# Sums over a head's rows, taken for four recurrence steps at once in TensorE's four column groups

## The chip, the cores and the metric

The kernel runs on one core of a Trainium2 chip. The time is that of one execution on the device, in microseconds (us). Engines are named as the profile names them: PE (TensorE, matmuls) and PEld (its weight loads), DVE (VectorE), ACT (ScalarE), POOL (GpSimd), SP (the engine that issues most DMAs). They run beside each other, each through its own list of instructions in order, and wait for each other on semaphores.

## The reference, cut to what matters

Two layers; the change is in the attention part of the first, a recurrence over 1024 tokens of 4 sequences, with 256 channels in 16 heads of N = 16:

```
r, k, v = xr @ Wr, xk @ Wk, xv @ Wv;  g = silu(xg @ Wg)
decay = exp(-exp(tdecay + tanh(xw @ td_w1) @ td_w2))
def step(S, inp):                       # S: one N x N matrix (i, j) for each head
    r_t, k_t, v_t, d_t = inp
    kv = k_t[..., :, None] * v_t[..., None, :]
    y = einsum('bhi,bhij->bhj', r_t, S + u[None, :, :, None] * kv)
    return d_t[..., None] * S + kv, y
mu, var = yh.mean(-1), yh.var(-1)       # over the 16 channels j of a head
yn = (yh - mu) / sqrt(var + EPS) * ln_w + ln_b
out = (yn * g) @ Wo
```

The sum over i, for each head and each j, is what the change deals with, and the mean over j that follows it.

## The kernel before, in words

Data lie with channels on the 128 partitions (CC = 2 blocks of P = 128 channels, 8 heads each) and the T = 1024 tokens of one sequence along the free dimension. A matmul takes at most W = 512 tokens, so there are BPB = 2 halves. The B = 4 sequences are run one after the other. S is never kept as a matrix: for a fixed block c and a fixed j, row (head, i) of S over all tokens is a scan on the partition (head, i). So a sequence has NJ = 32 recurrence steps (2 blocks, 16 values of j), 128 in all, numbered s. A step is made of:

- PE, `spread(s)` (L1089): two f32r matmuls put v of channel (head, j) on the 16 partitions of its head, into PSUM banks 0 and 1 or 2 and 3. It waits until the scan of step s-2 is done.
- DVE: kv = k * that, in PSUM (L1445), then the scan over the tokens (L1449) into one of the buffers of `st` (`state`), a ring of RING = 3. With s >= 3 the scan waits for `y_mm`, the sum that freed its buffer.
- POOL: state times r, in place (L1350, `pr_done`).
- PE, `y_sum(s)` (L1101): two fp32 matmuls, one for each half, with weights `sum_j[:, j, :]` (128 x 128) that add the 16 rows of each head into that head's channel j of banks 4 and 5. They hold 1 - 1/N in that column and -1/N in the others of the head, so the 16 steps of a block leave y less its mean over the head. At j = 15 two matmuls with `centre` (L1107) add the bonus term u*r*k*v, centred too.

An fp32 matmul stands in the trace as two MATMUL records and two weight loads.

Around the steps stands the side work, through banks 6 and 7 in turn (`side`, in the order of `USES`; a use waits until the one two before it has been read): the layernorm and mixes of the next sequence (`mean`, `var`, `bcast`, `xx`, `t5`, `m`, `td1`, `p`, `td2`), and behind each block's sums its group norm: `y` (ACT copies banks 4 and 5 to `y_`, L1284, and their square to `gsq`, L1285), `gvar` (variance), `gb` (1/std spread to the channels), and `wo` (output projection). The list `A_STEPS` gives, by hand, what each engine does in step s after its own part; `beside(b, n)` says which side work stands at step n of a sequence. All engines follow the same list. In step s PE does `y_sum(s-2)`, then `spread(s+1)`, then the side work; DVE does kv(s), the scan(s), then the side work.

A channel block stands inside permuted: first by half of j, then by head, then by j in the half (`by_parts`).

Of the kernel before, what the change touches and what calls it, by code (L numbers as in the profile page):

```python
# [10 lines left out]
P = 128  # L11
CC = C // P
NT = B * T
W = 512
# [4 lines left out]

HEADS, N = 16, 16  # L20
TM, TD = 32, 64
GN_EPS = 1e-5 * 8 ** 2
# [62 lines left out]
def adaln_kernel(nc, a, out):  # L85
# [40 lines left out]
    with ctx:  # L126
# [40 lines left out]
        def phase(spec):  # L167
# [16 lines left out]
            ("v_", [P, CC, T], fp32), ("v_parts", [P, CC, 2, T], f32r), ("decay", [P, CC, T], fp32),  # L184
            ("g_", [P, 2, CC, T], fp32), ("y_", [P, CC, T], fp32), ("gsq", [P, T], fp32), ("state", [P, 3, T + 1], fp32),
# [4 lines left out]
            ("spread", [P, N // 2, P], f32r), ("sum_j", [P, N, P], fp32),  # L190
            ("head_parts", [P, P], fp32), ("ident_a", [P, P], fp32), ("mean_parts", [P, P], fp32), ("centre", [P, P], fp32),
# [757 lines left out]
        V_MAA_X, V_DECAY, V_U, V_LNW, V_LNB = 5, 6, 7, 8, 9  # L949
        MIXES, NJ, RING = 5, CC * N, 3  # L950
        HALF_N = N // 2
# [21 lines left out]
        def beside(b, n):  # L973


            todo = []
            if n == 0:
                todo += both("td2", b, 1)
            if n == 1:
                if b:  # L980
                    todo += [("y", b - 1, 1)]
                todo += [("split", b, 1)]
            if b:
                todo += {3: [("gvar", b - 1, 1)], 4: [("gb", b - 1, 1, 0)], 5: [("gb", b - 1, 1, 1)],
                         9: both("wo", b - 1, 0), 10: both("wo", b - 1, 1)}.get(n, [])
# [15 lines left out]
        A_STEPS += [(b * NJ + n, beside(b, n)) for b in range(B) for n in range(NJ)]  # L1001
        A_STEPS += [(B * NJ, []), (B * NJ + 1, [("y", B - 1, 1)]), (None, [("gvar", B - 1, 1)]),
                    (None, both("gb", B - 1, 1)), (None, both("wo", B - 1, 0) + both("wo", B - 1, 1))]


        def reader(what):

            if what[0] == "p":
                return "V" if MIX_ORDER[what[2]][what[3]] == MIX_G else "A"
            return {"mean": "V", "var": "A", "bcast": "V", "t5": "A", "m": "V", "td1": "A", "td2": "A", "gvar": "A",  # L1010
                    "gb": "V", "wo": "V", "bonus": "V"}.get(what[0])
# [24 lines left out]
        def by_parts(ap):  # L1036

            return ap.rearrange("p (h x j) -> p x h j", x=2, j=HALF_N)

# [24 lines left out]
        def pe_a(pe):  # L1064
# [16 lines left out]
            def spread(s):  # L1081
                b, n = divmod(s, NJ)
                c, j = divmod(n, N)
                if s >= 2:
                    pe.wait_ge(scan_done, s - 1)
                if j == 0:
                    pe.wait_ge(lo_done_a, (b * CC + c + 1) * 2)
# [5 lines left out]

            def y_sum(s):
                b, n = divmod(s, NJ)
                c, j = divmod(n, N)
# [7 lines left out]
                if j == N - 1:  # L1104
                    wait_read(pe, ("bonus", b, c, 1))
                    for half in range(BPB):
                        ins = nc.tensor.matmul(bank(4 + half), a_["centre"][:, :], y_[:, c, half * W:(half + 1) * W],  # L1107
                                               start=False, stop=True, skip_group_check=True)
                    ins.then_inc(y_full, 1)

            def use(what):
# [49 lines left out]
                elif kind == "bonus":  # L1161
                    _, _, c, h = what
                    pe.wait_ge(rk_done, b * CC + c + 1)
                    ins = nc.tensor.matmul(side(what), a_["head_u"][:, c, :], y_[:, c, h * W:(h + 1) * W], start=True, stop=True)
                elif kind == "gvar":
                    c = what[2]
                    pe.wait_ge(y_copied, b * CC + c + 1)
                    for t in range(BT):
                        ins = nc.tensor.matmul(side(what)[:, t * (P // N):(t + 1) * (P // N)], gsq[:, t * P:(t + 1) * P],
                                               a_["mean_parts"][:, 0:P // 2:HALF_N], start=True, stop=True, skip_group_check=True)  # L1170
                elif kind == "gb":
# [28 lines left out]
        def act_a(act, own):  # L1200
            act.wait_ge(a_loaded, 16 * N_A_LOADS)
            for n in ("wv", "wg"):
                for k in range(CC):
                    for c in range(CC):
                        ins = nc.scalar.activation(a_[n][:, k, c * P:(c + 1) * P].rearrange(
                            "p (x h j) -> p x h j", x=2, j=HALF_N), by_parts(a_[n + "_in"][:, k, c * P:(c + 1) * P]), ACT.Copy)
            ins.then_inc(perm_read, 1)
# [7 lines left out]
            def do(what):  # L1215
# [65 lines left out]
                elif kind == "y":  # L1281
                    c = what[2]
                    act.wait_ge(y_full, b * CC + c + 1)
                    nc.scalar.activation(y_[:, c, :], bank2(4), ACT.Copy)  # L1284
                    nc.scalar.activation(gsq[:, :], bank2(4), ACT.Square).then_inc(y_copied, 1)  # L1285
                elif kind == "gvar":
# [3 lines left out]
                elif kind == "gb" and what[3] == 0:  # L1290

                    c = what[2]
                    act.wait_ge(rstd_done, RSTD["gvar", b, c])
                    for x in range(2):
                        to = gsq[:, :].rearrange("p (t x h j) -> p t x h j", x=2, h=P // N, j=HALF_N)[:, :, x, :, :]
                        ins = nc.scalar.activation(to, a_["gn_rs"][:, :, :].unsqueeze(3).broadcast_to(
                            [P, BT, P // N, HALF_N]), ACT.Copy)
                    ins.then_inc(widened, 1)
                elif kind == "gb":
# [55 lines left out]
        def dve_a(dve, own):  # L1355
            dve.wait_ge(a_loaded, 16 * N_A_LOADS)
            dve.wait_ge(h_zero, 1)
            parts = dict(x=2, h=P // N, j=HALF_N)
            nc.vector.tensor_copy(a_["ident_parts"][:, :].rearrange("p (x h j) -> p x h j", **parts),
                                  by_parts(a_["ident_a"][:, :])).then_inc(maps_done, 1)  # L1360
            for x in range(2):
                nc.vector.tensor_copy(a_["ident_twice"][:, x * (P // 2):(x + 1) * (P // 2)].rearrange(
                    "p (h j) -> p h j", j=HALF_N), by_parts(a_["ident_a"][:, :])[:, 0, :, :]).then_inc(maps_done, 1)
            heads, in_parts = a_["head_ones"][:, 0:P:N], a_["head_parts"][:, :]
            own.link(nc.vector.tensor_copy(in_parts.rearrange("p (x h j) -> p x h j", **parts), by_parts(a_["head_ones"][:, :])))

            own.link(nc.vector.tensor_scalar(a_["sum_j"][:, :, :], in_parts.unsqueeze(1).broadcast_to([P, N, P]), -1.0 / N, None,
                                             ALU.mult))
            for j in range(N):
                first = j // HALF_N * (P // 2) + j % HALF_N  # L1370
                ins = nc.vector.tensor_scalar(a_["sum_j"][:, j, first:first + P // 2 - HALF_N + 1:HALF_N], heads, 1.0 - 1.0 / N, None, ALU.mult)
            ins.then_inc(fixed_done, 1)
# [62 lines left out]
            for s, todo in A_STEPS:  # L1435
                if s is not None and s < B * NJ:
# [1042 lines left out]
```

## Time and profile before

| | us |
|---|---|
| median of 3 runs | 5319.94 (5316.01 to 5320.66) |
| the profiled execution, its own time | 5312.82 |
| its span, first to last instruction | 5311.0 |
| granted clock of PE, mean | 0.953 |
| the 128 steps | from 178 to 853 |

The page of the profile gives busy time by engine and by slice of the span. The views by window, by group of instructions and in order of time give the stretch from 178 to 853 us, in which the recurrence stands. The rest of the span belongs to other parts of the two layers, which the change leaves as they are.

### The profile page before, as it was taken

What the parts mean: (1) busy time and instruction counts of PE and PEld (TensorE: products, weight loads), DVE (VectorE), ACT (ScalarE), POOL (GpSimd) and SP (SyncE); (2) the same over time, 40 slices, a digit from 0 to 9 for tenths busy, and PEclk for the clock granted to TensorE, in tenths of its full rate; (3) what the DMA queues carried; (4) which work ended last, traced back from release to release, by engine and by line L of the source; (5) the groups of instructions that cost most, each with busy time, mean ns of one, the idle gap of its engine ahead of it and who ended that gap; (6) DMA issues with size and microseconds to landing.
All of it is one profiled execution on the core that took longest, in us unless ns stands there. A gap on an engine that the chain in (4) does not pass through costs nothing. (4 is left out here: it accounts for less than half of the span.)

```text
span 5311.0 us, 84166 instructions
## 1 busy us (share of the span) xinstructions
PE 4578.8 (86%) x28586; PEld 2382.0 (45%) x28586; DVE 4038.4 (76%) x6600; ACT 3406.8 (64%) x2365; POOL 3149.1 (59%) x2722
## 2 busy tenths in 40 slices
PE   5999987786589988888898888898988888399999
PEld 3344443473234434344344343443443434277777
DVE  2688886524499999999999999999999998522221
ACT  1221211211599999999999999999999996334443
POOL 0566563420477777777777777777777774133333
PEclk8899998898799999999999999999999998699999
DMA  6000001351100000000000000000000000200000
GB/s 217 0 0 0 0 0 44 116 183 69 46 3 2 4 2 2 18 2 3 3 2 4 16 2 4 2 4 2 11 4 2 2 4 3 96 8 16 8 16 8
DMA packets 71211, 123.45 MB, mean 23 GB/s; under 512 B 8231, under 2 KB 46727, under 8 KB 68032
## 3 DMA queue, kind: packets, MB, share of 16 engines
q1 hardware_dynamic: 61888, 98.94, 5.6%
q0 software_dynamic: 9216, 23.17, 1.2%
q8 instruction: 57, 0.93, 0.1%
q14 instruction: 50, 0.41, 0.0%
HBM read 67.39 MB, written 61.03 MB: 24 GB/s over the span
## 5 line engine op out<-in xcount | busy, mean ns | idle before, releaser
L892 DVE CUSTOM_DVE_ANT_0 e_slots<-e_slots,banks 128x1024 f32<-128x1024 f32 x2048 | 2445.6, 1216 | 104.3 <-PE banks L577 99.9
L660 ACT ACTIVATE e_slots<-e_slots 128x4096 f32<-128x4096 f32 x512 | 1841.1, 3620 | 75.5 <-DVE e_slots L847 50.9
L577 PE MATMUL banks<-ex_parts,sel 128*128 128x512 f32 x4096 | 1520.4, 454 | 159.5 <-DVE ew L892 153.1
L536 PE MATMUL banks<-e_slots,w_score 128*32 128x256 f32 x16384 | 1256.2, 399 | 175.3 <-ACT e_slots L660 168.8
L744 POOL TENSOR_SCALAR e_slots<-k,qt 128x1024 f32<-128x1024 f32 x896 | 1002.9, 1121 | 672.4 <-DVE ew L892 631.2
L750 POOL TENSOR_SCALAR e_slots<-e_slots,qt 128x1024 f32<-128x1024 f32 x896 | 1000.3, 1124 | 64.5 <-POOL e_slots L744 25.7
L577 PEld LDWEIGHTS banks<-ex_parts,sel 128*128 128x128 f32 x4096 | 632.4, 190 | 904.3 <-DVE ew L892 733.2
L536 PEld LDWEIGHTS banks<-e_slots,w_score 128*32 128x32 f32 x16384 | 375.9, 110 | 873.0 <-issue 567.6
L651 ACT ACTIVATE e_slots<-k,qt 128x1024 f32<-128x1024 f32 x512 | 570.6, 1139 | 4.6 <-DVE ew L892 4.4
L2190 POOL TENSOR_TENSOR g_l<-tmp,g_h 128x512 fp32r<-128x512 f32 x192 | 248.8, 1296 | 437.4 <-ACT g_h L2157 307.0
L847 DVE TENSOR_SCALAR e_slots<-k,qt 128x1024 f32<-128x1024 f32 x640 | 466.3, 792 | 0.5 <-POOL qt L754 0.5
L1350 POOL TENSOR_TENSOR state<-state,r_ 128x1024 f32<-128x1024 f32 x128 | 290.0, 2267 | 223.6 <-DVE state L1449 223.2
L2070 PE MATMUL banks<-g_h,r_h 128*128 128x512 f32 x1024 | 410.3, 401 | 0.9 <-POOL g_l L2190 0.9
L2070 PE MATMUL banks<-g_l,r_h 128*128 128x512 f32 x1024 | 404.4, 395 | 0.0
L1449 DVE TENSOR_TENSOR_SCAN state<-decay,banks 128x1024 f32<-128x1024 f32 x128 | 292.7, 2287 | 4.4
L1101 PE MATMUL banks<-state,sum_j 128*128 128x512 f32 x512 | 255.2, 621 | 37.3 <-POOL state L1350 31.4
L2156 ACT ACTIVATE tmp<-banks,r_sh 128x512 f32<-128x512 f32 x128 | 88.2, 689 | 267.8 <-PE banks L2070 267.7
L2237 DVE SCALAR_TENSOR_TENSOR xr<-banks,r_s3g,xr 128x512 f32<-128x512 f32 x16 | 11.3, 747 | 269.1 <-PE banks L2070 269.1
L2070 PEld LDWEIGHTS banks<-g_h,r_h 128*128 128x128 f32 x1024 | 192.2, 188 | 51.0 <-issue 3.3
L2070 PEld LDWEIGHTS banks<-g_l,r_h 128*128 128x128 f32 x1024 | 192.2, 188 | 49.3 <-issue 3.3
L667 ACT ACTIVATE ex<-banks,negmax 128x512 f32<-128x512 f32 x128 | 88.2, 689 | 185.6 <-DVE negmax L864 185.6
L2216 DVE RECIPROCAL r_std<-r_std 128x512 f32<-128x512 f32 x8 | 26.8, 3353 | 224.9 <-ACT r_std L2126 224.9
(313 smaller groups left out, 5234.3 us busy)
## 6 DMA issues: line engine op xcount, KB each, us to landing
moe_slots<-empty_slot SPq DMA_DIRECT2D x1, 10320.0 KB, 47.3
slots<-moe_slots SPq DMA_DIRECT2D x8, 1290.0 KB, 6.3
moe_out<-empty_slot SPq DMA_DIRECT2D x1, 8192.0 KB, 67.9
two_rows<-moe_out SPq DMA_DIRECT2D x16, 512.0 KB, 6.5
stage<-in_h SPq DMA_DIRECT2D x8, 1024.0 KB, 4.8
x_tokens<-in_x SPq DMA_DIRECT2D x1, 4096.0 KB, 13.9
w_down<-in_w_down SPq DMA_DIRECT2D x1, 4096.0 KB, 12.3
x_between<-x_tokens SPq DMA_DIRECT2D x8, 512.0 KB, 4.8
```

Of the source, the lines that this page charges most:

```text
L536: ins = nc.tensor.matmul(banks[TI * g:TI * (g + 1), par, side * QW:(side + 1) * QW], c_["w_score"][:, s, half, :], e_slots[:, par, COLG * ...
L577: ins = nc.tensor.matmul(spread[n % 2][:, half * W:(half + 1) * W], c_["sel"][:, half, n, :], ex_parts[:, par, :], start=True, stop=True)
L651: nc.scalar.activation(e_slots[:, par, n, :], k2[:, :], ACT.Relu, bias=qt[:, par, 0, place(n):place(n) + 1]).then_inc(z_a, 1)
L660: nc.scalar.activation(e_slots[:, par, four, :], e_slots[:, par, four, :], ACT.Sqrt, bias=EPS_RHO).then_inc(sqrt_done, 1)
L744: nc.gpsimd.tensor_scalar(e_slots[:, par, n, :], k2[:, :], FLT_MAX, qt[:, par, 1, place(n):place(n) + 1], ALU.min, ALU.max).then_inc(z_cla ...
L750: nc.gpsimd.tensor_scalar(e, e, qt[:, par, 0, place(n):place(n) + 1], 1.0, ALU.add, ALU.mult).then_inc(z_p, 1)
L847: nc.vector.tensor_scalar(e_slots[:, par, n, :], k2[:, :], qt[:, par, 0, place(n):place(n) + 1], 0.0, ALU.add, ALU.max).then_inc(z_v, 1)
L892: nc.vector.tensor_tensor_reduce(out=e, in0=e, in1=spread[n % 2], scale=1.0, scalar=0.0, op0=ALU.mult, op1=ALU.add, accum_out=ew[:, q, pla ...
L1101: ins = nc.tensor.matmul(bank(4 + half), a_["sum_j"][:, j, :], st[:, s % RING, half * W:(half + 1) * W], start=j == 0, stop=False, skip_gr ...
L1350: nc.gpsimd.tensor_tensor(state, state, r_[:, b % 2, n // N, :], ALU.mult).then_inc(pr_done, 1)
L1449: nc.vector.tensor_tensor_scan(st[:, s % RING, 1:T + 1], dk[:, c, :], kv, 0.0, ALU.mult, ALU.add).then_inc(scan_done, 1)
L2070: ins = nc.tensor.matmul(dst, w_[w][:, k, o * P:(o + 1) * P], x[:, k, :], start=k == 0 and part_ == 0, stop=k == n_k - 1 and part_ == 1)
```

## The change

- `RING` goes from 3 to 6. `sum_j` (128 x 16 x 128) is replaced by `sum_4` (128 x 4 x 4 x 8): weights of 32 columns, ones in the 8 columns of slot i, for i from 0 to 3.
- The 16 values of j are taken in the order 0, 4, 8, 12, 1, 5, 9, 13, ... (`J_ORDER`), so that four steps in a row belong to the four quarters of the j.
- `y_sum` is replaced by `y_sums`, which runs after every fourth step. For each half it issues four fp32 matmuls, one for each of the four steps' states, of 32 output columns each, into partitions 0-31, 32-63, 64-95 and 96-127 of bank 4 or 5. The scan waits for the sum of its ring's group of four.
- The permuted order of channels becomes j first, then head. The set-up copies, `ident_parts`, `mean_parts`, and the widening of `gn_rs` (one ACTIVATE of 1024 instead of two of 512) follow it.
- The sums no longer take away the mean. The bonus term is added with `ident_a` instead of `centre`, and a new side use `cen` (two for each block) multiplies the copied y with `centre`; ACT takes the square of the result into `gsq` and copies it back to `y_`. `y` is now one ACTIVATE. `cen` stands at steps 2 and 18; `gvar` moves from 3 and 19 to 4 and 20, `gb` from 4, 5, 20, 21 to 5, 6, 21, 22.

```diff
+RING = 6
-"state", [P, 3, T + 1]            -"sum_j", [P, N, P]
+"state", [P, RING, T + 1]         +"sum_4", [P, 4, 4, P // N]
...
+        GROUP = 4
+        J_ORDER = [N // GROUP * g + i for i in range(N // GROUP) for g in range(GROUP)]
...
-                todo += {3: [("gvar", b - 1, 1)], 4: [("gb", b - 1, 1, 0)], 5: [("gb", b - 1, 1, 1)],
+                todo += {2: both("cen", b - 1, 1), 4: [("gvar", b - 1, 1)], 5: [("gb", b - 1, 1, 0)], 6: [("gb", b - 1, 1, 1)],
...
-                     17: [("y", b, 0)], 19: [("gvar", b, 0)], 20: [("gb", b, 0, 0)], 21: [("gb", b, 0, 1)]}.get(n, [])
+                     17: [("y", b, 0)], 18: both("cen", b, 0), 20: [("gvar", b, 0)], 21: [("gb", b, 0, 0)], 22: [("gb", b, 0, 1)]}.get(n, [])
...
-            return ap.rearrange("p (h x j) -> p x h j", x=2, j=HALF_N)
+            return ap.rearrange("p (h j) -> p j h", j=N)
...
-            def y_sum(s):
+            def y_sums(s):
...
                 pe.wait_ge(pr_done, s + 1)
-                if j == 0 and s:
+                if i == GROUP - 1 and s >= N:
                     pe.wait_ge(y_copied, s // N)
+                onto = a_["sum_4"][:, i // GROUP, :, :].rearrange("p i h -> p (i h)")
                 for half in range(BPB):
-                    ins = nc.tensor.matmul(bank(4 + half), a_["sum_j"][:, j, :], st[:, s % RING, half * W:(half + 1) * W],
-                                           start=j == 0, stop=False, skip_group_check=True)
+                    for g in range(GROUP):
+                        ins = nc.tensor.matmul(banks[g * 32:(g + 1) * 32, 4 + half, :], onto,
+                                               st[:, (s - GROUP + 1 + g) % RING, half * W:(half + 1) * W],
+                                               start=i == GROUP - 1, stop=False, skip_group_check=True)
                 ins.then_inc(y_mm, 1)
...
-                        ins = nc.tensor.matmul(bank(4 + half), a_["centre"][:, :], y_[:, c, half * W:(half + 1) * W],
+                        ins = nc.tensor.matmul(bank(4 + half), a_["ident_a"][:, :], y_[:, c, half * W:(half + 1) * W],
...
+                elif kind == "cen":
+                    _, _, c, h = what
+                    pe.wait_ge(y_copied, b * CC + c + 1)
+                    ins = nc.tensor.matmul(side(what), a_["centre"][:, :], y_[:, c, h * W:(h + 1) * W], start=True, stop=True)
                 elif kind == "gvar":
-                    pe.wait_ge(y_copied, b * CC + c + 1)
+                    wait_read(pe, ("cen", b, c, 1))
...
-                if s is not None and s >= 2:
-                    y_sum(s - 2)
+                if s is not None and s >= 2 and (s - 2) % GROUP == GROUP - 1:
+                    y_sums(s - 2)
...
-                    nc.scalar.activation(y_[:, c, :], bank2(4), ACT.Copy)
-                    nc.scalar.activation(gsq[:, :], bank2(4), ACT.Square).then_inc(y_copied, 1)
+                    nc.scalar.activation(y_[:, c, :], bank2(4), ACT.Copy).then_inc(y_copied, 1)
+                elif kind == "cen":
+                    _, _, c, h = what
+                    cols = slice(h * W, (h + 1) * W)
+                    wait_mm(act, what)
+                    nc.scalar.activation(gsq[:, cols], side(what), ACT.Square)
+                    nc.scalar.activation(y_[:, c, cols], side(what), ACT.Copy).then_inc(side_a, 1)
...
+            own.link(nc.vector.memset(a_["sum_4"][:, :, :, :], 0.0))
+            for i in range(4):
+                ins = nc.vector.tensor_copy(a_["sum_4"][:, i, i, :], heads)
...
                     if s >= RING:
-                        dve.wait_ge(y_mm, s - RING + 1)
+                        dve.wait_ge(y_mm, (s - RING) // GROUP + 1)
```

## Rows read from the trace of the kernel before

**Rows 1.** The page: busy time by engine over the whole span.
```profile
PE 4578.8 (86%) x28586; PEld 2382.0 (45%) x28586; DVE 4038.4 (76%) x6600; ACT 3406.8 (64%) x2365; POOL 3149.1 (59%) x2722
```

**Rows 2.** By window: length, busy by engine (instructions), clock, DMA share, GB/s.
```profile
178.00:853.00 675.00, 611.26 (x1675) 283.10 (x1675) 561.08 (x413) 138.38 (x193) 421.72 (x187) 0.96 0.00 0
...
820.00:840.00 20.00, 14.25 (x35) 6.31 (x36) 19.83 (x12) 0.00 (x0) 13.34 (x7) 1.00 0.00 0
```

**Rows 3.** DVE's groups, 178 to 853: busy, mean ns, idle before, releaser.
```profile
L1449 DVE TENSOR_TENSOR_SCAN state<-decay,banks 128x1024 f32<-128x1024 f32 x128 | 292.7, 2287 | 4.4
L1445 DVE TENSOR_TENSOR banks<-k_,banks 128x1024 f32<-128x1024 f32 x128 | 155.5, 1215 | 9.2 <-PE banks L1089 9.2
L1406 DVE SCALAR_TENSOR_TENSOR xmix<-banks,vecs,xx 128x512 f32<-128x512 f32 x60 | 44.6, 748 | 30.2 <-PE banks L1140 21.3 <-PE banks L1142 6.5
...
L1427 DVE TENSOR_TENSOR y_<-y_,banks 128x512 f32<-128x512 f32 x14 | 9.4, 672 | 16.6 <-PE banks L1176 16.6
L1432 DVE SCALAR_TENSOR_TENSOR x_tokens<-banks,mod,x_tokens 128x512 f32<-128x512 f32 x12 | 8.9, 742 | 9.6 <-PE banks L1182 9.6
L1413 DVE SCALAR_TENSOR_TENSOR g_<-th_g,banks 128x512 f32<-128x512 f32 x12 | 8.2, 687 | 18.0 <-ACT th_g L1248 18.0
L1386 DVE TENSOR_TENSOR xmix<-x_tokens,banks 128x1024 f32<-128x1024 f32 x6 | 7.3, 1221 | 12.4 <-PE banks L1116 12.4
L1393 DVE TENSOR_TENSOR xmix<-xmix,banks 128x1024 f32<-128x1024 f32 x6 | 7.3, 1212 | 6.0 <-PE banks L1126 6.0
...
L1390 DVE RECIPROCAL ln_rs<-ln_sd 128x4 f32<-128x4 f32 x6 | 1.1, 178 | 9.9 <-ACT ln_sd L1222 9.9
```

**Rows 4.** In order of time: a step with `p`, then one with `m`.
```profile
310.39 1.03 PE L1089 MATMUL banks<-v_parts,spread 128*128 128x512 f32 x2
...
311.26 3.60 PE L1155 MATMUL banks<-xmix,wv 128*128 128x512 f32 x8
...
314.70 1.88 PE L1101 MATMUL banks<-state,sum_j 128*128 128x512 f32 x4
...
316.97 1.98 PE L1140 MATMUL banks<-t5a,w2r 32*128 32x512 f32 x4
...
318.13 1.61 DVE L1406 SCALAR_TENSOR_TENSOR xmix<-banks,vecs,xx 128x512 f32<-128x512 f32 x2 [1.39 <-PE banks L1140]
...
324.60 1.88 PE L1101 MATMUL banks<-state,sum_j 128*128 128x512 f32 x4
```

**Rows 5.** In order of time: a step with no side work.
```profile
825.27 2.37 POOL L1350 TENSOR_TENSOR state<-state,r_ 128x1024 f32<-128x1024 f32 x1 [1.45 <-DVE state L1449]
...
826.34 2.29 DVE L1449 TENSOR_TENSOR_SCAN state<-decay,banks 128x1024 f32<-128x1024 f32 x1
...
827.68 1.98 PE L1101 MATMUL banks<-state,sum_j 128*128 128x512 f32 x4 [1.36 <-POOL state L1350]
...
829.79 2.29 DVE L1449 TENSOR_TENSOR_SCAN state<-decay,banks 128x1024 f32<-128x1024 f32 x1
```

**Rows 6.** PE's groups by line, whole run: the sums.
```profile
L1101 PE MATMUL banks<-state,sum_j 128*128 128x512 f32 x512 | 255.2, 621 | 37.3 <-POOL state L1350 31.4 <-ACT gsq L1285 5.6
```

**Rows 7.** In order of time, second layer: matmuls of 32 columns in four column groups.
```profile
2500.46 0.64 PE L536 MATMUL banks<-e_slots,w_score 128*32 128x256 f32 x8
2501.03 0.74 PE L577 MATMUL banks<-ex_parts,sel 128*128 128x512 f32 x2
```

**Rows 8.** In order of time: PE waits for POOL, then its clock is down.
```profile
739.26 3.78 PE L1101 MATMUL banks<-state,sum_j 128*128 128x512 f32 x4 [2.68 <-POOL state L1350]
742.05 1.84 PE L1089 MATMUL banks<-v_parts,spread 128*128 128x512 f32 x2
...
745.23 0.69 DVE L1427 TENSOR_TENSOR y_<-y_,banks 128x512 f32<-128x512 f32 x1 [4.26 <-PE banks L1176]
```

**Rows 9.** In order of time: one `g_` pair, waits of DVE.
```profile
341.81 0.69 DVE L1413 SCALAR_TENSOR_TENSOR g_<-th_g,banks 128x512 f32<-128x512 f32 x1 [1.03 <-ACT th_g L1248]
```

**Rows 10.** In order of time: the square behind the last step.
```profile
856.44 1.02 ACT L1285 ACTIVATE gsq<-banks 128x1024 f32<-128x1024 f32 x1
```

More of the change, by code:

```diff
@@ L184, in adaln_kernel @@
             ("v_", [P, CC, T], fp32), ("v_parts", [P, CC, 2, T], f32r), ("decay", [P, CC, T], fp32),
-            ("g_", [P, 2, CC, T], fp32), ("y_", [P, CC, T], fp32), ("gsq", [P, T], fp32), ("state", [P, 3, T + 1], fp32),
+            ("g_", [P, 2, CC, T], fp32), ("y_", [P, CC, T], fp32), ("gsq", [P, T], fp32), ("state", [P, RING, T + 1], fp32),
             ("t5a", [P, W], fp32), ("t5b", [TM, W], fp32), ("tw", [TD, BPB, W], fp32), ("th_g", [P, CC, W], fp32),
@@ L189, in adaln_kernel @@
             ("wg", [P, CC, C], fp32), ("wo", [P, CC, C], fp32), ("vecs", [P, 10, CC], fp32),
-            ("spread", [P, N // 2, P], f32r), ("sum_j", [P, N, P], fp32),
+            ("spread", [P, N // 2, P], f32r), ("sum_4", [P, 4, 4, P // N], fp32),
             ("head_parts", [P, P], fp32), ("ident_a", [P, P], fp32), ("mean_parts", [P, P], fp32), ("centre", [P, P], fp32),
@@ L949, in adaln_kernel @@
         V_MAA_X, V_DECAY, V_U, V_LNW, V_LNB = 5, 6, 7, 8, 9
-        MIXES, NJ, RING = 5, CC * N, 3
+        MIXES, NJ = 5, CC * N
+        GROUP = 4
+        J_ORDER = [N // GROUP * g + i for i in range(N // GROUP) for g in range(GROUP)]
         HALF_N = N // 2
@@ L1001, in adaln_kernel @@
         A_STEPS += [(b * NJ + n, beside(b, n)) for b in range(B) for n in range(NJ)]
-        A_STEPS += [(B * NJ, []), (B * NJ + 1, [("y", B - 1, 1)]), (None, [("gvar", B - 1, 1)]),
+        A_STEPS += [(B * NJ, []), (B * NJ + 1, [("y", B - 1, 1)]), (None, both("cen", B - 1, 1) + [("gvar", B - 1, 1)]),
                     (None, both("gb", B - 1, 1)), (None, both("wo", B - 1, 0) + both("wo", B - 1, 1))]
@@ L1009, in reader @@
                 return "V" if MIX_ORDER[what[2]][what[3]] == MIX_G else "A"
-            return {"mean": "V", "var": "A", "bcast": "V", "t5": "A", "m": "V", "td1": "A", "td2": "A", "gvar": "A",
+            return {"mean": "V", "var": "A", "bcast": "V", "t5": "A", "m": "V", "td1": "A", "td2": "A", "cen": "A", "gvar": "A",
                     "gb": "V", "wo": "V", "bonus": "V"}.get(what[0])
@@ L1082, in spread @@
                 b, n = divmod(s, NJ)
-                c, j = divmod(n, N)
+                c, i = divmod(n, N)
+                j = J_ORDER[i]
                 if s >= 2:
                     pe.wait_ge(scan_done, s - 1)
-                if j == 0:
+                if i == 0:
                     pe.wait_ge(lo_done_a, (b * CC + c + 1) * 2)
@@ L1164, in use @@
                     ins = nc.tensor.matmul(side(what), a_["head_u"][:, c, :], y_[:, c, h * W:(h + 1) * W], start=True, stop=True)
+                elif kind == "cen":
+                    _, _, c, h = what
+                    pe.wait_ge(y_copied, b * CC + c + 1)
+                    ins = nc.tensor.matmul(side(what), a_["centre"][:, :], y_[:, c, h * W:(h + 1) * W], start=True, stop=True)
                 elif kind == "gvar":
                     c = what[2]
-                    pe.wait_ge(y_copied, b * CC + c + 1)
+                    wait_read(pe, ("cen", b, c, 1))
                     for t in range(BT):
                         ins = nc.tensor.matmul(side(what)[:, t * (P // N):(t + 1) * (P // N)], gsq[:, t * P:(t + 1) * P],
-                                               a_["mean_parts"][:, 0:P // 2:HALF_N], start=True, stop=True, skip_group_check=True)
+                                               a_["mean_parts"][:, 0:P // N], start=True, stop=True, skip_group_check=True)
                 elif kind == "gb":
@@ L1205, in act_a @@
                         ins = nc.scalar.activation(a_[n][:, k, c * P:(c + 1) * P].rearrange(
-                            "p (x h j) -> p x h j", x=2, j=HALF_N), by_parts(a_[n + "_in"][:, k, c * P:(c + 1) * P]), ACT.Copy)
+                            "p (j h) -> p j h", j=N), by_parts(a_[n + "_in"][:, k, c * P:(c + 1) * P]), ACT.Copy)
             ins.then_inc(perm_read, 1)
@@ L1293, in do @@
                     act.wait_ge(rstd_done, RSTD["gvar", b, c])
[L1294 to L1298, printed above, removed]
+                    nc.scalar.activation(gsq[:, :].rearrange("p (t j h) -> p t j h", t=BT, j=N), a_["gn_rs"][:, :, :].unsqueeze(2)
+                                         .broadcast_to([P, BT, N, P // N]), ACT.Copy).then_inc(widened, 1)
                 elif kind == "gb":
@@ L1357, in dve_a @@
             dve.wait_ge(h_zero, 1)
-            parts = dict(x=2, h=P // N, j=HALF_N)
-            nc.vector.tensor_copy(a_["ident_parts"][:, :].rearrange("p (x h j) -> p x h j", **parts),
+            nc.vector.tensor_copy(a_["ident_parts"][:, :].rearrange("p (j h) -> p j h", j=N),
                                   by_parts(a_["ident_a"][:, :])).then_inc(maps_done, 1)
@@ L1362, in dve_a @@
                 nc.vector.tensor_copy(a_["ident_twice"][:, x * (P // 2):(x + 1) * (P // 2)].rearrange(
-                    "p (h j) -> p h j", j=HALF_N), by_parts(a_["ident_a"][:, :])[:, 0, :, :]).then_inc(maps_done, 1)
+                    "p (j h) -> p j h", j=HALF_N), by_parts(a_["ident_a"][:, :])[:, 0:HALF_N, :]).then_inc(maps_done, 1)
             heads, in_parts = a_["head_ones"][:, 0:P:N], a_["head_parts"][:, :]
[L1365 to L1371, printed above, removed]
+            own.link(nc.vector.tensor_copy(in_parts.rearrange("p (j h) -> p j h", j=N), by_parts(a_["head_ones"][:, :])))
+            own.link(nc.vector.memset(a_["sum_4"][:, :, :, :], 0.0))
+            for i in range(4):
+                ins = nc.vector.tensor_copy(a_["sum_4"][:, i, i, :], heads)
             ins.then_inc(fixed_done, 1)
```

4 lines of the change are left out of this document (2 added, 2 removed).

## The prediction

> **What bounds the kernel now.** I began with the page [rows 1]: PE is the busiest engine over the whole span. That says little here, because the change touches one stage only. The view by window gives that stage, the 128 steps, as 675 us [rows 2]: PE is busy for 611.3 us of them (91%), DVE for 561.1 (83%), POOL for 421.7 (62%), ACT for 138.4 (21%). The clock is at 0.96 and no DMA runs. So two engines are close to the bound, and the question is which of them ends the steps.
>
> The view in order of time answers it twice. With no side work, one scan starts 3.45 us after the other (826.34 to 829.79), which is the scan's 2.29 and the product's 1.22 and nothing between them [rows 3, 5]: DVE is the bound, and the sums (1.98 us) lie beside it. With side work it is the other way round. The sum of one step starts at 314.70 and the same one of the next pair at 324.60, so a pair of steps with a `p` and an `m` takes 9.9 us, and in it DVE waits 1.39 us for the matmuls of `m` [rows 4]. PE has no gap in that pair. I work its time out from starts: the `p` matmuls run from 311.26 to 314.70, so eight records take 3.44 us, 0.43 each. Four records (a sum, an `m`) then take 1.72, two (a spread) 0.86. The pair is 2 x 1.72 (sums) + 2 x 0.86 (spreads) + 1.72 (`m`) + 3.44 (`p`) = 10.3 us, near those 9.9. DVE's work for the pair is 2 x 3.50 + 2 x 0.75 = 8.5 us.
>
> So the end of the stage is DVE's: its 561.1 us of work plus 113.9 us of idle time. The groups by line say what it waited for [rows 3]: `m` 30.2, `g` 18.0, `gb` 16.6, `mean` 12.4, `ln_rs` 9.9, `wo` 9.6, the products 9.2, `bcast` 6.0 and 2 for the rest. Most of them are matmuls of the side work that stand in PE's list behind a `y_sum`. The change can give back no more than this idle time, since it takes no work from DVE inside the steps.
>
> **The change, part by part.**
>
> *The sums.* Before, 128 steps x 4 records x 0.43 = 220 us of PE. After, 32 calls of `y_sums`, each with 16 records of 128x512 on 32 columns. The nearest row is a matmul of the second layer with the same 32 columns, fp32 too, four column groups in a row: eight records of 256 elements start at 2500.46, and the next matmul starts at 2501.03, 0.57 us on [rows 7]. One after the other they would have taken 8 x 0.215 = 1.7 (half of the 0.43 of 512 elements each). So the groups do run together. At 512 elements I add two passes of 0.215 for the longer rows (1.0 us a half) or double the whole (1.14). A call is thus 2.0 to 2.3 us, and I take 2.3; the bound on the other side is 16 x 0.43 = 6.9 us, if nothing overlaps. 32 x 2.3 = 74 us, so 146 us leave PE.
>
> The Trainium skill, "TensorEngine Tiling (Array Packing)", Performance Considerations, promises up to four times for output columns of 32 or fewer, and its Key Properties say that a change of tiling mode drains the engine. Without any such drain a call would be 1.72 us and with it about what I take; the trace's 0.57 in place of 0.43 for the eight records agrees with a cost of this kind.
>
> *Waits of the sums.* Each `y_sum` waits for POOL's product, and `spread` and the side work are queued behind it on PE. PE lost 31.4 us that way and 5.6 us to the copy of the banks [rows 6]; once, POOL was late behind its `split`, PE stood 2.68 us, and DVE then 4.26 us at `gb` [rows 8]. Afterwards three steps in four have no such wait. In the fourth the order is the same as before. In a step without side work, POOL's product is ready about 2.5 us after its scan (827.68 less the scan's end at 825.2) [rows 5]; with 2.3 for the call and 0.86 for the spread that makes 5.7 us, and the product that needs the spread is due after 6.9. So the burst fits, with 1.2 us to spare. The ring of six adds no wait of its own: scan 4k+6 waits for the call that PE issues ahead of the very spread that its product needs.
>
> *`cen`.* Eight blocks x 4 records x 0.43 = 14 us more on PE, and for ACT four ACTIVATEs of 512 elements in place of one of 1024, at 21% busy. The bonus matmul keeps its size and only gets other weights. In the steps PE's sum is 611 - 146 + 14 = 479 us. On the chain, `cen` stands between `y` and `gvar`, which is moved one step later, where it meets `t5`; `gb` follows in steps that have `m` work. I put 0 to 2 us on each of the 8 blocks and take 2.5 in all. No DMA and no other queue is moved past.
>
> *Behind the last step* nothing covers `cen`. It adds 0.86 and some 0.3 of latency, and two times two ACTIVATEs of about 0.6 (half of 1.02, with its fixed part), and takes away the square of 1024 elements, 1.02 [rows 10]: 1 to 4 us, I take 3.
>
> *Set-up.* The fill of `sum_j` on DVE goes. It lay beside PE's permutations and the load of x, which end later, so it is worth nothing, with 0 to 1 us lost if the new strided copies on ACT are slower.
>
> *What DVE still waits for.* In the `p` and `m` pair PE now has 10.3 - 3.44 + half of 2.3 = 8.0 us against DVE's 8.5, so DVE bounds it. `m` keeps 8 of 30 (behind `t5`, and beside `wo`). `g`: the second of each pair waits for two matmuls and the tanh whatever PE did before, 1.03 in the row [rows 9], six pairs; with something for the first, 7.5 of 18 stay. `gb` 6 of 16.6. `mean` 3 of 12.4. `ln_rs` 5 of 9.9, as a chain of square, `var` and a table load is longer than one step. `wo` 6 of 9.6: around it four steps hold 22.6 us of PE against 20.2 of DVE. The products 8 of 9.2, since 7.7 of it is the very first start. `bcast` 2 of 6.0, the rest its 2, and 2.5 come new with `cen`. These are judged, not measured; together 50 stay and 64 go.
>
> *The clock.* Now PE is busy 14.25 of 20 us even where there is no side work, and the clock is 1.00 [rows 2]. After the change only a spread (0.86) stands in three of four such steps of 3.45 us. Where PE had stood for 2.68 us behind small matmuls the four records took 3.78 instead of 1.98 us and the spread 1.84 instead of 1.03 [rows 8]: the lower level, 1.2 GHz. I expect that in the stretches without side work. At 1.2 GHz a call takes 4.6 at most and a spread 1.72, so 2.5 + 4.6 + 1.7 = 8.8 against 6.9: a stall of 1 to 2 us in each group of four. About five groups of the last sequence and one in each of the others stand so: 8 x 1.5 = 12 us, or none if the clock holds. I take 10.
>
> "TensorE: Matmul & The Clock Gate", HAM oscillation, in the Trainium skill speaks against the change in the same way: gaps in PE's work send it to half rate. By it the stretches named would all be slow and the sum as I have it; without it, 10 us better.
>
> **Sum:** -64 + 10 + 3 = -51 us. Against the profiled execution's own 5312.8 us that is 5261.8. The median of the runs is 7.1 us above that execution, so the forecast is 5269 us for the median.
>
> **Rivals.**
> - *All waits go.* DVE runs without idle time but for the first start and the tail: 114 - 8 - 9 (its other fixed chains, `g` above all) = 97 less 3, so about 5226. For: in the last plain steps it does just that. Against: the chains over ACT. A gain between this and mine, 5226 to 5250, has a good chance.
> - *The waits are the chains' own.* If the side work of each step is late from its own round trip over ACT and POOL and not from the sum ahead of it, only the 37 us of PE's waits [rows 6] come through, in part: some 20 to 25 us, 5297. Against: PE has no gap in the pair of rows 4.
> - *The four column groups don't run together.* With 512 elements in two banks, or because the two records of an fp32 matmul follow each other in the same group, a call takes up to 6.9 us. From 3.5 us (6.9 - 2.5 - 0.86) it decides against DVE's pace in plain steps; at 6.9 each call holds DVE for 3.3 us there, about 10 groups, 33 us; PE's sum rises by 14 for `cen`, which it passes on where it is the bound; with 3 for the tail, about +45: 5365. This is the slower case. Against it stands the 0.57 of [rows 7]; 6%. At half overlap, 3.5 to 4.5 us, nothing changes in sign.
> - *A clock that stays down* also where there is side work would put 16 us of PE against 8.5 in a pair. The records of such a pair run at 0.43 each, the upper level, where PE is busy without a gap [rows 4], and in the pair it stays 94% busy; so at most in parts, a gain of 10 us or none: 5310.
>
> **How the numbers follow.** My forecast with its neighbourhood (5250 to 5288): 0.48. A larger gain (5220 to 5250): 0.22. Chains' own waits (5288 to 5309): 0.16. Clock down or small gain (5309 to 5331): 0.07. Slower (above 5331): 0.07. 0.2% is 10.6 us, about what a measurement of this kernel can tell from no change: faster below 5309.3, 0.86; the same 0.07; slower 0.07. The range takes 5222 to 5305, which leaves out 0.02 below and some 0.17 above.
>
> **What would show it.** The 128 steps take about 615 us (603 to 640 by the range). DVE's busy time in them stays near 561 and its idle time falls to about 55. A call of `y_sums` has 16 records in 2.0 to 2.3 us at full clock. `m` waits nearly vanish, and the second wait of each `g_` pair stays at 1.0. PE's clock falls below 0.9 in the last sequence. Wrong would be: a call above 3.5 us, DVE's product waiting for its spread behind a call in most groups, scans waiting for `y_mm`, or new waits at `gb` above 2 us a block.

## The result, and the profile after

The changed kernel takes 5339.36 us in the median of 7 runs (5331.51 to 5348.01), the kernel before 5320.66 (5310.2 to 5323.65) on the same chip: a ratio of 1.0037, with a 95% interval of 1.0026 to 1.0049. It is slower by 0.4%, where 1% faster was forecast. On another chip it was 1.0029 (1.0017 to 1.0040). The profiled execution, the slowest of the seven, has a span of 5346.3 us against 5311.0. 10.9 of those 35.3 us lie behind phase B's first matmul, in the part that the change leaves alone; no run says why.

First the stage by window, as in [rows 2]; the stretches go from the first scan's start to the last one's end, for the whole stage and for the last sequence alone. The kernel after:

```profile
184.70:868.90 684.20, 534.60 (x1688) 228.60 (x1686) 560.12 (x413) 153.86 (x213) 421.24 (x186) 0.82 0.00 0
...
732.20:868.90 136.70, 87.51 (x297) 38.07 (x296) 117.50 (x77) 17.32 (x23) 84.43 (x38) 0.71 0.00 0
```

The kernel before, the same two stretches:

```profile
178.20:849.30 671.10, 608.81 (x1670) 282.16 (x1669) 560.91 (x412) 138.38 (x193) 419.38 (x186) 0.96 0.00 0
...
722.30:849.30 127.00, 101.00 (x288) 48.53 (x287) 117.11 (x77) 15.08 (x19) 84.07 (x38) 0.97 0.00 0
```

DVE's work is the same (560.9 and 560.1 us) and the stage is 13.1 us longer, so all of the loss there is idle time of DVE. PE lost 74 us of busy time, not the 132 forecast. The clock column says why: 0.96 became 0.82, and in the last sequence 0.97 became 0.71. The last sequence, which has little side work, is 9.7 us longer although PE has less to do in it.

From here on I measure a version, in one profiled execution, by the distance between the starts of its first and its last scan: 668.8 us before (sequences 175.8, 184.0, 184.3 and 124.7), 681.9 after (176.3, 184.3, 186.8 and 134.5). A second profile of the changed kernel gave 680.5 us, with sequences up to 2.6 us apart, so a difference of that size between two versions says nothing. Two more pieces stand around the steps: the first scan starts at 184.7 instead of 178.2, and from the last scan's start to phase B's first matmul it is 38.0 instead of 33.2 us.

The call of `y_sums` is near what was forecast (2.0 to 2.3 us). In order of time, one at full clock and one in the last sequence:

```profile
304.42 1.93 PE L1108 MATMUL banks<-state,sum 128*32 128x512 f32 x16
...
843.14 3.64 PE L1108 MATMUL banks<-state,sum 128*32 128x512 f32 x16 [1.79 <-POOL state L1364]
...
846.71 1.82 PE L1094 MATMUL banks<-v_parts,spread 128*128 128x512 f32 x4
...
847.97 1.23 DVE L1456 TENSOR_TENSOR banks<-k_,banks 128x1024 f32<-128x1024 f32 x1 [1.01 <-PE banks L1094]
```

Sixteen records of 32 columns take 1.93 us, so the four groups do run together: apart they would take 6.9. At the lower level they take 3.64, and then the spread behind them is late and DVE waits 1.01 us for it.

DVE's idle time by group, to be laid beside [rows 3]:

```profile
L1456 DVE TENSOR_TENSOR banks<-k_,banks 128x1024 f32<-128x1024 f32 x128 | 155.5, 1215 | 14.4 <-PE banks L1094 14.4
L1417 DVE SCALAR_TENSOR_TENSOR xmix<-banks,vecs,xx 128x512 f32<-128x512 f32 x60 | 44.5, 747 | 32.3 <-PE banks L1148 27.6 <-PE banks L1150 3.2
...
L1438 DVE TENSOR_TENSOR y_<-y_,banks 128x512 f32<-128x512 f32 x14 | 9.4, 669 | 7.0 <-PE banks L1188 7.0
...
L1424 DVE SCALAR_TENSOR_TENSOR g_<-th_g,banks 128x512 f32<-128x512 f32 x12 | 8.1, 682 | 13.4 <-ACT th_g L1260 13.4
L1397 DVE TENSOR_TENSOR xmix<-x_tokens,banks 128x1024 f32<-128x1024 f32 x6 | 7.3, 1221 | 21.2 <-PE banks L1124 21.2
```

`gb` gave back 9.6 us, as meant, and `g` 4.6 of the 10.5 meant. But `mean` went from 12.4 to 21.2, the products from 9.2 to 14.4, `bcast` from 6.0 to 9.0, and `m`, which should have given back 22, stands at 32.3 where it had 30.2. `gn_rs`, the reciprocal behind `gvar`, went from 1.3 to 7.3 and `ln_rs` from 9.9 to 13.1. The scan itself waits 4.4 us in all before and after, so the ring of six and its waits for `y_mm` cost nothing.

### The profile page after: what moved, and what is told of

Read it like the earlier page. It is cut to its first block and busy times, and to the rows that moved or that the text cites. A ratio compares the mean times of both kernels' runs of the same rounds, so it can differ in the third digit from the quotient of the medians.

```text
span 5346.3 us, 84253 instructions
## 1 busy us (share of the span) xinstructions
PE 4522.7 (85%) x28618; PEld 2334.6 (44%) x28618; DVE 4036.7 (76%) x6588; ACT 3425.0 (64%) x2387; POOL 3151.5 (59%) x2722
## 5 line engine op out<-in xcount | busy, mean ns | idle before, releaser
L1094 PE MATMUL banks<-v_parts,spread 128*128 128x512 f32 x256 | 114.6, 536 | 91.3 <-DVE state L1460 86.1
## 6 DMA issues: line engine op xcount, KB each, us to landing
x_tokens<-in_x SPq DMA_DIRECT2D x1, 4096.0 KB, 14.1
```

## What the two traces suggest

**The clock (theory C).** `mean` stands at the head of a sequence, behind three steps with hardly any work for PE. In order of time, the kernel after:

```profile
356.52 1.21 PE L1094 MATMUL banks<-v_parts,spread 128*128 128x512 f32 x2 [2.71 <-DVE state L1460]
...
359.96 1.22 PE L1094 MATMUL banks<-v_parts,spread 128*128 128x512 f32 x2 [2.24 <-DVE state L1460]
...
361.11 3.78 PE L1168 MATMUL banks<-tw,td 64*128 64x512 f32 x4
...
364.82 3.78 PE L1124 MATMUL banks<-x_tokens,ones_mean 128*128 128x512 f32 x4
...
368.64 1.22 DVE L1397 TENSOR_TENSOR xmix<-x_tokens,banks 128x1024 f32<-128x1024 f32 x1 [5.29 <-PE banks L1124]
```

PE issued two records and then stood for 2.2 to 2.7 us, in each of these steps, and four records of `td2` and of `mean` now take 3.78 us each, against 1.98 before the change. DVE waits 5.29 us for the second. Before the change the sums filled those gaps. Theory C says that the freed PE pays for itself with a low clock, and more work on PE would be faster.

**The order (theory Q).** `cen` and the moved `gvar` and `gb` put new round trips on the chains. Step 23 takes 9.4 to 10.1 us from scan to scan, against 6.15 before:

```profile
315.35 1.24 ACT L1316 ACTIVATE y_<-y_,ln_half 128x1024 f32<-128x1024 f32 x1 [10.74 <-DVE y_ L1438]
...
316.53 0.75 DVE L1417 SCALAR_TENSOR_TENSOR xmix<-banks,vecs,xx 128x512 f32<-128x512 f32 x1 [1.21 <-PE banks L1148]
316.61 1.28 ACT L1251 ACT_TABLE_LOAD   x1
...
317.90 0.59 ACT L1251 ACTIVATE tw<-banks 64x512 f32<-64x512 f32 x1
318.55 1.64 PE L1148 MATMUL banks<-t5a,w2r 32*128 32x512 f32 x2 [2.06 <-ACT tw L1251]
...
320.22 0.75 DVE L1417 SCALAR_TENSOR_TENSOR xmix<-banks,vecs,xx 128x512 f32<-128x512 f32 x1 [2.94 <-PE banks L1148]
```

The second `gb` now shares step 22 with `td1`. ACT can take `td1`'s result only after its affine step, which waits for DVE's `gb`, and after a table load of 1.28 us; the bank that it holds is the one that the second `m` matmul needs. So DVE waits for PE, PE for ACT, and ACT for DVE, 4.2 us of DVE in all. Theory Q says that this order is the loss, and that a freed PE is worth what was forecast.

## The experiments

Where an experiment adds work, it is this: fp32 matmuls of 128x512 with zero weights, added into banks 4 and 5, so that the sums stay as they are.

**The part alone: three of four sums left out of the kernel before.** No `cen`, the old order; the output lacks those terms.

```diff
             def y_sum(s):
...
+                if j % 4 != 3:
+                    return
                 pe.wait_ge(pr_done, s + 1)
...
-                        dve.wait_ge(y_mm, s - RING + 1)
+                        dve.wait_ge(pr_done, s - RING + 1)
+                        if s - RING + 1 >= 4:
+                            dve.wait_ge(y_mm, (s - RING + 1) // 4)
```

> The kernel before the change with the sums of three of four steps left out (j = 3, 7, 11, 15 remain, two matmuls of 128x512 each, as before), so y lacks three quarters of its terms; no cen, the old order, a ring of three. It shows what freeing PE of the sums does alone. C: the clock of the steps falls to 0.80 to 0.87 and first to last scan only from 669 to 645 to 665 us, time 5295 to 5315. Q: DVE's waits behind the sums go, scans over 605 to 625 us, time 5255 to 5275, as forecast for the whole change.

Measured: 5313.2 us, 1.0004 (0.9994 to 1.0013) of the kernel before. The view by window, whole stage and last sequence:

```profile
176.90:842.10 665.20, 526.51 (x1288) 249.88 (x1286) 558.02 (x412) 138.94 (x193) 418.43 (x186) 0.79 0.00 0
709.00:842.10 133.10, 83.78 (x193) 43.27 (x192) 117.62 (x77) 15.19 (x19) 84.01 (x38) 0.69 0.00 0
```

PE is rid of 192 matmuls, and nothing comes of it: 662.9 us from first to last scan, 5.9 less than before, and the last sequence takes 130.8 instead of 124.7. Q's forecast of 5255 to 5275 is out; C's scans and time came true, with a clock of 0.79 just under its 0.80 to 0.87. This is the plainest answer to where the gain went, since the rest of the change is not in this kernel.

**The changed kernel with its sums apart.** Each step's sum in its own step, in one column group.

```diff
-                if s is not None and s >= 2 and (s - 2) % GROUP == GROUP - 1:
+                if s is not None and s >= 2:
...
+                g = i % GROUP
                 for half in range(BPB):
-                    for g in range(GROUP):
+                    ins = nc.tensor.matmul(banks[g * 32:(g + 1) * 32, 4 + half, :], onto,
+                                           st[:, s % RING, half * W:(half + 1) * W],
+                                           start=i < GROUP, stop=False, skip_group_check=True)
```

> The changed kernel, but each step's sum is issued in its own step as before the change, as two fp32 matmuls of 32 columns in one column group, so no four run together; cen, the order and the ring of six stay. C: PE is as busy as before the change, the clock is above 0.93, and the time is that of before plus 14 us of PE for cen and 3 for the tail, 5325 to 5335, with scans over 670 to 680. Q: the order costs as it does in the changed kernel and PE's sums come on top, 5350 or more, scans over 695 or more.

Measured: 5340.64 us, 1.0055 (1.0038 to 1.0072), clock 0.95 in the stage, 687.2 us from first to last scan. It lies between the two forecasts: the time is above C's and the scans below Q's 695. Against the kernel before, this version has as many records for the sums (of 32 columns now), the new set-up and order of j, the ring, `cen` and its order, at nearly the same clock (0.95 and 0.96), and its scans need 18.4 us more. 9.1 us of that are step 23 of the first three sequences, and 5.2 the last sequence. So both theories hold a part. Taking the sums together then saves 5.3 us (687.2 to 681.9), about the 5.9 of the part alone.

**The old order.** `gvar` and `gb` back at their steps, `cen` where it is.

```diff
-                todo += {2: both("cen", b - 1, 1), 4: [("gvar", b - 1, 1)], 5: [("gb", b - 1, 1, 0)], 6: [("gb", b - 1, 1, 1)],
+                todo += {2: both("cen", b - 1, 1), 3: [("gvar", b - 1, 1)], 4: [("gb", b - 1, 1, 0)], 5: [("gb", b - 1, 1, 1)],
...
-                     17: [("y", b, 0)], 18: both("cen", b, 0), 20: [("gvar", b, 0)], 21: [("gb", b, 0, 0)], 22: [("gb", b, 0, 1)]}.get(n, [])
+                     17: [("y", b, 0)], 18: both("cen", b, 0), 19: [("gvar", b, 0)], 20: [("gb", b, 0, 0)], 21: [("gb", b, 0, 1)]}.get(n, [])
```

> The changed kernel with gvar and gb put back to the steps at which they stood before the change (gvar 3 and 19, gb 4, 5, 20, 21; cen stays at 2 and 18). C: no change that matters, 5335 to 5345, clock 0.82. Q: the waits at step 23 (9.4 to 10.1 us from scan to scan, 6.15 before the change) go back to about 6, 3.5 us in each of three sequences, and the time falls by 10 to 15 us to about 5326.

Measured: 5315.49 us, 1.0006 (0.9996 to 1.0015), the same as the kernel before; 665.3 us from first to last scan, 16.6 less than the changed kernel, at the same clock of 0.82. Step 23 takes 4.76 us in each of the three sequences, 15.0 us less in all. The other steps of those three are 2.5 us longer together, and the last sequence, which has no `td1`, is 4.2 us shorter. So the collision is most of what the order costs, and not all. DVE's wait for `m` falls from 32.3 to 19.5 us and the one at `gn_rs` goes; the one at `gb` rises from 7.0 to 10.8. Q is right on the order, by more than it said.

**PE filled in every step.** Two zero-weight matmuls at the end of PE's step, in the three of four steps without a call.

```diff
+            def fill(s, halves):
+                start = (s - 2) % N < GROUP - 1
+                for half in range(halves):
+                    nc.tensor.matmul(bank(4 + half), a_["zero_w"][:, :], a_["wo"][:, :, :].rearrange("p k c -> p (k c)"),
+                                     start=start, stop=False, skip_group_check=True)
...
                         use(what)
+                if s is not None and 2 <= s < B * NJ and (s - 2) % GROUP != GROUP - 1:
+                    fill(s, 2)
```

> The changed kernel, with two fp32 matmuls of 128x512 with zero weights into banks 4 and 5 at the end of PE's step in each step that has no call of y_sums (nothing is left out; zeros are added). It gives PE back about the busy time that the change took from it, but behind the side work instead of ahead of it. Theory C (the clock: PE, freed, falls to 1.2 GHz and its matmuls on DVE's chains take twice as long): the granted clock of the 128 steps rises from 0.82 to above 0.93, first to last scan falls from 682 to 640 to 655 us, and the time is 5290 to 5315. Theory Q (the order of the side work: cen, and gvar and gb moved onto steps with t5 and td1): the clock rises too, but the scans stay at 680 or more and the time at 5335 to 5350.

Measured: 5378.5 us, 1.0126 (1.0109 to 1.0143), and 719.7 us from first to last scan. C's 5290 to 5315 is out, and the time is above Q's 5350 too, but the sequences differ. The first three take 597.7 us instead of 547.4: DVE's wait for `m` rises from 32.3 to 58.9 us and that for `gb` from 7.0 to 19.0, while the products wait less (11.0 for 14.4). The added matmuls stand in PE's list ahead of the next step's side work. The last one takes 122.0 us instead of 134.5:

```profile
774.60:898.90 124.30, 105.49 (x392) 46.94 (x390) 116.78 (x77) 17.21 (x23) 84.52 (x38) 0.97 0.00 1
```

PE has 18 us more to do in it than in the changed kernel, the clock is 0.97 instead of 0.71, and it is 12.4 us shorter. That suggests that the fill has to stand in the gaps only, which the next version tries.

**PE filled in light steps only.** The same call under one more condition: the side work of the step has less than 1 us for PE (steps 3, 30 and 31 of a sequence, and most of the last). `PE_US` is a table of the side work's PE time: `p`, `wo`, `t5`, `mean`, `td1` 1.7 us, `var`, `gvar` 1.8, `bcast`, `gb` 1.1, `m`, `cen`, `bonus`, `td2` 0.86.

```diff
-                if s is not None and 2 <= s < B * NJ and (s - 2) % GROUP != GROUP - 1:
+                if (s is not None and 2 <= s < B * NJ and (s - 2) % GROUP != GROUP - 1
+                        and sum(PE_US.get(w[0], 0) for w in todo) < 1.0):
```

> The changed kernel with the two zero-weight fp32 matmuls of 128x512 at the end of PE's step only where PE has next to no side work (steps 3, 30 and 31 of a sequence and most of the last sequence), nothing left out. In the run with them in all steps the last sequence took 122.0 us between scans against 134.5 in the changed kernel, and the first three 597.7 against 547.4. C (the low clock costs time by itself): the last sequence takes 120 to 126 us, the first three fall to 535 to 545 because mean and the first uses of a sequence meet a warm PE, and the time is 5315 to 5328. Q (only the order costs; more PE work can only delay): the last sequence stays above 130, time 5335 or more.

Measured: 5311.29 us, 1.0000 (0.9991 to 1.0010); 659.0 us from first to last scan, sequences 173.7, 182.1, 183.5 and 119.7. That is 22.9 us less than the changed kernel, by added work alone. The clock of the last sequence is 0.94, and the idle time ahead of `mean` fell from 21.2 to 11.8 us. C holds, with a time 4 us better than its range.

**Light steps filled, and the old order**, the last edit and that of the old order together.

> The same zero-weight matmuls in light steps, with gvar and gb at their old steps (5315.5 without the matmuls). C: the two gains add, last sequence 118 to 124, time 5292 to 5305, faster than the kernel before the change. Q: 5312 to 5320, as without them.

Measured: 5297.68 us, 0.9981 (0.9971 to 0.9991); 649.1 us from first to last scan. The time is in C's range. Of the two gains, 16.6 and 22.9 us, 32.8 are there together: they add in the main, and not wholly.

**The steps with `m`, `cen` or `bonus` alone filled too** (the bound 1.0 becomes 1.8).

> As the one before, with zero-weight matmuls also in the steps whose only side work on PE is the two matmuls of m, cen or bonus (1.7 us). C, if the low clock also holds the m and p steps: 5285 to 5300, below the light version. If PE's own order is tight there, as in the run with them in all steps: 5305 to 5325, above it. Q: above 5315.

Measured: 5286.76 us, 0.9955 (0.9938 to 0.9971): 0.45% faster than the kernel before, within C's range. First to last scan 640.5 us, clock 0.92:

```profile
177.10:819.90 642.80, 565.28 (x1876) 243.26 (x1874) 558.89 (x412) 145.50 (x207) 418.94 (x186) 0.92 0.00 1
```

**The part alone, with light steps filled.** The kernel before with three of four sums left out (as above, so its output lacks them) and the matmuls of zero weight.

> The kernel before the change with three of four sums left out (y lacks those terms; 5313.2) and the zero-weight matmuls in light steps. It asks what the freed PE is worth when the clock is held in the light steps. C: last sequence from 130.8 back to 118 to 124, the first three from 532 to 515 to 525, time 5285 to 5300. Q, or chains over ACT and POOL as the limit: 5308 to 5318.

Measured: 5287.42 us, 0.9955 (0.9941 to 0.9969), against 1.0004 without the fill. First to last scan 643.4 instead of 662.9; the last sequence 122.4 instead of 130.8. What frees PE is worth 5.9 us on this stage when the clock is left to itself and 25.4 us when it is held up in the light steps. The kernel before as it is, with the same fill, was not run; its clock in the stage is 0.96 already, but what the fill would give there is open.

**The changed kernel again, and a fill ahead of the first scan.** The first scan's start had fallen on two values: 175.5 to 178.2 in the kernel before and five versions, 184.0 to 185.3 in the changed kernel and three versions. (The expectation below miscounts them.)

> The changed kernel once more, on the chip that also runs the next one. Before its first scan it issues the same matmuls in the same order as the kernel before the change; the first scan stood at 178.2 us there, at 184.7 in it, and in seven variants at 175.5 to 178.0 four times... and at 184.0 to 185.3 three times, in both families. If that is the chance of where the clock rises, this run may show either value and no other; if it belongs to the change's set-up, it is 184 to 185 again. Time 5325 to 5345 by both theories.

Measured: 5334.66 us; first scan at 175.0, first to last scan 680.5. So the first scan's 6.5 us are no part of the change, and its loss in the stage repeats, 11.7 us after 13.1.

```diff
+                if s is None and todo[0][0] in ('mean', 'xx') and todo[0][1] == 0:
+                    for k in range(1 if todo[0][0] == 'mean' else 3):
+                        fill(2, 1)
```

> The best version so far (gvar and gb at their old steps, zero-weight matmuls in light and middling steps, 5286.8) with the same kind of matmul also ahead of the first scan: one behind each of the first two mean and three behind each of the first two xx, where PE waits 2 to 6 us and the clock is 0.77. C: the low clock costs time there too; first scan at 168 to 174 us instead of 175 to 185, time 5275 to 5283. If those matmuls only get in the way: first scan at 180 or later, 5288 or more.

Measured: 5293.06 us, 0.9948 (0.9930 to 0.9965), with the chip's kernel before at 5319. The first scan starts at 171.1, and the clock from 60 us to there is 0.88 instead of 0.72 to 0.78. The first scan's start is what C said. The time is not: 5293 misses the expected 5275 to 5283 by 10 us, where the kernel before is slower by 6 on this chip. In the profile the scans take the 640.5 us of the version without this fill, and the part behind phase B's first matmul, with no fill in it, is 13.7 us longer; that is left open. In ratio it is the fastest version, but its interval overlaps that of the other.

## Why the prediction was wrong

**What bounds the stage**: right. DVE's 561 us of work stayed (560.1), and time was won and lost in its idle time alone.

**The sums**: right. A call takes 1.93 us, under the 2.0 to 2.3 of the forecast.

Three terms of the sum failed. For the stage it had -64 for the waits and +10 for the clock, -54 us, and the profile showed +13.1. Of the 67.1 us between them, 14.8 are the clock's (24.8 that the fill gives back, less the 10), 16.6 the order's, and 35.7 are left for the waits, with `cen` and the rest of the low clock in them.

**The clock, sized too small.** Its direction and its mechanism were right, its size and its reach wrong. I priced it at 10 us, in stretches without side work, by calls that delay their spread. The last sequence alone is 9.8 us longer, but 5.2 of that stand in the version with the sums apart too, at a clock of 0.95. What I left out is that the same low clock is carried into the work behind a light stretch: DVE's wait at `mean`, at the head of each sequence, rose from 12.4 to 21.2 us, and light steps filled bring it back to 11.8. Those records take twice as long (3.78 us for 1.98), and DVE waits for them. With the light and middling steps filled the stage falls by 24.8 us (665.3 to 640.5), and with the light ones alone by 22.9, 16.2 and 19.5 us in three kernels. So the term was 16 to 25 us, where I had 10. It is probably more, since the clock was still 0.92 and the fill takes PE's time; no run held the clock at 0.96 with the sums together. From the Trainium skill, "TensorE: Matmul & The Clock Gate", HAM oscillation, I had weighed against the change that gaps in PE's work bring it to half rate. The trace agrees, with 3.64 us for a call in the last sequence, though the page tells of longer waits, for DMA, and here gaps of 2.2 to 2.7 us went with the lower level.

**`cen` and the order, sized too small.** "0 to 2 us on each of the 8 blocks and take 2.5 in all" was 18.4 us at nearly equal clock (the version with the sums apart), of which the order is 16.6 (the old order). Most of it is one collision, three times, `gb` and `td1` in step 22. I had looked at `gvar` beside `t5` and had not followed who holds the two side banks: I counted PE's time for each step, and the loss is a chain through three engines, one after the other; ACT's three instructions alone are 3.1 us of it. Behind the last step the piece is 4.8 us longer, where I took 3. Both the clock and `cen` have a part in it. Without `cen` it takes 33.2 us in the kernel before and 32.9 in the filled version, with the clock in it at 0.79, and 36.4 with three of four sums left out, where it is 0.68. With `cen` it takes 35.7 and 36.0 where the clock in it is 0.86, and 37.3 to 39.6 in the other versions, where it is 0.74 to 0.78.

**The waits that were to go: the largest.** 64 us were to go. With the clock at 0.92 and the old order, 28.3 us have gone from the stage (668.8 to 640.5), and DVE still waits for `gb` 14.1, `m` 16.4, `g` 11.6, `mean` 11.5, `bcast` 9.6 and `ln_rs` 9.3 us, against 6, 8, 7.5, 3, 2 and 5 as judged. `m` and `g` gave back part; `gb`, `mean` and `ln_rs` barely moved from [rows 3], and `bcast` rose. I had called these waits PE's, because the view names PE as the last releaser. In this version PE itself stands still ahead of some of the matmuls in question, for its own inputs:

```profile
L1140 PE MATMUL banks<-xmix,maa_w 128*128 128x512 f32 x24 | 22.2, 1081 | 12.6 <-DVE xmix L1420 12.6
...
L1188 PE MATMUL banks<-ident_a,gsq 128*128 128x128 f32 x112 | 17.4, 304 | 6.0 <-ACT gsq L1319 6.0
```

These are `t5`, which waits 12.6 us for DVE, and `gb`, which waits 6.0 us for ACT. PE also waits 36.8 us there for the scans ahead of its spreads, so it is not short of time. That points to the rival "the waits are the chains' own", which I gave 0.16: its "some 20 to 25 us" of gain are near the 25.4 and 28.3 that the stage gave back with the clock held. No run takes a link out of one of these chains, so this part is argued and not shown. How the rest divides between chains, the fill's own time and the remaining low clock, the runs do not tell.

**Together**: the order and `cen` +18.4, the sums together -5.3 (net of the clock), which is the stage's +13.1, and the end +4.8; that makes 18 us, and the medians differ by 18.7. That they are so close is partly luck, as the parts come from one profiled execution each and the executions of the changed kernel lie up to 16 us apart. The forecast for the sums together was -64 + 10. The rival on the slower side that I named (groups that don't run together) didn't happen; it went slower by two mechanisms that each had a term in my sum, at a fraction of its size.

## What to carry to other kernels

Where an engine is taken off work that lay beside the bound, ask what that work did besides: here it kept PE at the upper clock for the chains that the bound does wait for. Before a batch of short matmuls is made cheaper, look at the granted clock and at PE's gaps in the stretches that would be left empty; if they empty, matmuls of zero weight in them can be worth more than the saving (19.5 us here against 5.9), provided they stand only where there is a gap.
When side work is moved by a step, follow each shared buffer through all engines, not only the load of each engine in each step.

## What the runs showed of the hardware

- Four groups of 32 output columns, fp32, 512 elements, two halves: 16 records in 1.93 us at the upper level and 3.64 at the lower, against 1.98 for four records of 128 columns.
- Two records and then 2.2 to 2.7 us without work, in turn, had the clock at 1.2 GHz (records twice as long: 3.78 us for four instead of 1.98). With two zero-weight matmuls in the same steps the clock of the last sequence went from 0.69 to 0.72 without them to between 0.86 and 0.97. Their weights were zero and the streamed operand was not; matmuls with zero weights kept it up.
- The same instructions up to the first scan took 175.0 in one execution of the changed kernel and 184.7 us in another; the clock from 60 us on was 0.78 and 0.73. So a single profile of this kernel cannot tell a gain of under 10 us in that stretch, where PE often waits.
